# The end of the experts and the first tiles of dense attention rearranged, with result-row gathers that skip rows outside their class

## The reference, cut to what matters

```python
# first layer, feed-forward: 32 experts, 4 of them for each token, capacity 512
order = argsort(flat_ids); pos = arange(N) - starts[sorted_eid]
buf = zeros((E, C, 512)).at[sorted_eid, pos].set(x[tok], mode='drop')
g, u = split(einsum('ech,ehf->ecf', buf, w13))
eo = einsum('eci,eih->ech', silu(g) * u, w2)
routed = zeros_like(x).at[tok].add(eo[sorted_eid, pos] * flat_w[order][:, None])
shared = silu(x @ shared_gate_w) * (x @ shared_up_w) @ shared_down_w
x = x + routed + shared                     # beside the residual of its input norm
# second layer: q, k, v of 16 heads of 128, causal softmax, output projection
x = x + attention(layernorm(x), W_Q, W_K, W_V, W_O, b_Q, b_K, b_V, b_O)
```

## Time and profile before

| | us |
|---|---|
| Median of 3 runs | 3078.67 |
| Their range | 3078.39 to 3084.72 |
| The traced execution, its own time | 3087.53 |
| Its span, first to last instruction | 3086.1 |
| Mean granted TensorE clock | 0.967 |
| PE busy, share of the span | 94% |

### The profile page before, as it was taken

One profiled execution on the slowest core, in us unless ns is written; L12 is line 12 of the kernel. 1 busy time (PEld: TensorE's weight loads), 2 busy tenths in 40 slices (PEclk: granted clock), 3 DMA queues, 4 the chain that ended last, 5 costly groups with the idle time before them and its releaser, 6 DMA issues.

```text
span 3086.1 us, 46590 instructions
## 1 busy us (share of the span) xinstructions
PE 2887.0 (94%) x16712; PEld 1971.4 (64%) x16745; DVE 2055.0 (67%) x3792; ACT 1595.0 (52%) x2971; POOL 1138.1 (37%) x1152
## 2 busy tenths in 40 slices
PE   8899998899998889999996999999999999989998
PEld 3344443444443548888865888888888888856665
DVE  3554445699986877777776445656555566549998
ACT  2223222288887537777752444444456455437764
POOL 2343243334422033333345445454544444323310
PEclk9899999799999889999997999999999999989999
DMA  3000000000000238865673013222122234120000
GB/s 132 1 1 1 1 1 1 8 6 6 3 2 21 80 139 331 326 247 192 213 222 98 21 32 84 63 57 68 49 90 88 81 115 134 35 89 8 15 15 21
DMA packets 125913, 238.83 MB, mean 77 GB/s; under 512 B 14283, under 2 KB 73248, under 8 KB 119285
## 3 DMA queue, kind: packets, MB, share of 16 engines
q1 hardware_dynamic: 102020, 119.95, 12.1%
q0 software_dynamic: 22512, 113.80, 10.7%
q10 hardware_dynamic: 1152, 2.10, 0.2%
HBM read 223.99 MB, written 40.63 MB: 86 GB/s over the span
## 4 chain that ended last, share of the span: by engine, by line
PE 55%; DVE 13%; issue 7%; ACT 6%; POOL 3%; DMA 1%; SPq 0%; POOLq 0%; ACTq 0%; DVEq 0%; another core or an unknown queue 0%
PE ps L1651 9%; PE ps L1653 9%; PE ps L1652 9%; PE ps L901 3%; PE ps L890 3%; PE ps L2918 2%; DVE ps L2493 2%; PE ps L879 2%; PE ps L2928 2%; DVE b_mx L1023 1%; PE ps L2893 1%; ACT d_PTh L2355 1%; PE ps L1665 1%; ACT d_qk L2340 1%; DVE d_PTl L2507 1%
## 5 line engine op out<-in xcount | busy, mean ns | idle before, releaser
L2693 POOL TENSOR_SCALAR d_P<-d_P,d_rv 128x128 f32<-128x128 f32 (+3 forms) x256 | 289.8, 1144 | 553.2 <-DVE d_rv L2500 552.9
L1023 DVE TENSOR_REDUCE b_mx<-ps 128x1 f32<-128x512 f32 x512 | 320.8, 683 | 31.7 <-PE ps L879 28.1
L964 ACT ACTIVATE b_PT<-ps 128x512 f32<-128x512 f32 x512 | 277.6, 601 | 45.0 <-PE ps L890 43.5
L2348 ACT ACTIVATE d_P<-ps,d_nb 128x128 f32<-128x128 f32 (+3 forms) x256 | 135.2, 528 | 219.0 <-DVE d_nb L2493 217.7
L2507 DVE TENSOR_TENSOR d_PTl<-ps,d_PTh 128x384 fp32r<-128x384 f32 (+1 forms) x192 | 114.6, 597 | 157.4 <-ACT d_PTh L2355 157.4
L1651 PE MATMUL ps<-d_xh,d_wh 128*128 128x512 f32 x512 | 210.1, 410 | 1.5 <-DVE d_xl L2467 1.4
L1652 PE MATMUL ps<-d_xl,d_wh 128*128 128x512 f32 x512 | 204.1, 399 | 0.0
L1653 PE MATMUL ps<-d_xh,d_wl 128*128 128x512 f32 x512 | 203.9, 398 | 0.0
L879 PE MATMUL ps<-b_KT,b_Q 64*128 64x512 f32 x512 | 201.0, 475 | 2.1 <-DVE b_mx L1023 1.0
L890 PE MATMUL ps<-b_Q,b_KT 64*128 64x512 f32 x512 | 187.1, 452 | 0.5
L476 ACT ACTIVATE a_P<-ps 128x2048 f32<-128x2048 f32 (+1 forms) x48 | 76.4, 1592 | 210.0 <-PE ps L340 183.0
(11 more groups left out here) (485 smaller groups left out, 8456.3 us busy)
## 6 DMA issues: line engine op xcount, KB each, us to landing
eoscr<-x_eo SPq DMA_DIRECT2D x87, 256.0 KB, 4.3
d_w<-in_L_attn_W_Q SPq DMA_DIRECT2D x32, 256.0 KB, 3.9
d_w<-in_L_attn_W_K SPq DMA_DIRECT2D x32, 256.0 KB, 4.7
d_w<-in_L_attn_W_V SPq DMA_DIRECT2D x32, 256.0 KB, 5.4
d_wo<-in_L_attn_W_O SPq DMA_DIRECT2D x16, 512.0 KB, 4.7
d_cmb<-in_wgT SPq DMA_DIRECT2D x16, 512.0 KB, 5.0
d_cmb<-in_wuT SPq DMA_DIRECT2D x16, 512.0 KB, 4.7
d_cmb<-in_wdT SPq DMA_DIRECT2D x16, 512.0 KB, 4.2
```

What stands on the lines that cost most here:

```text
L964: e.activation(M.PT[:, half, v % 2, 2 * p + y, :], ps[:, O.bank(("ex", v, y)), :], ACT.Exp, scale=0.25).then_inc(S["b_ex"], 1)
L1023: e.tensor_reduce(M.mx[:, r % 2, q, h:h + 1], ps[:, O.SCORES[O.score(t, h) % 3], :], AX.X, ALU.max).then_inc(S["b_mx"], 1)
L2693: e.tensor_scalar(P, P, M.rv[:, y, q:q + 1], None, ALU.mult).then_inc(S["d_nm"], 1)
```

## The change

Index handling: `late_rows` adds 65536 to each index that is outside its class (`M.far`), and each of the 21 class gathers gets a bounds check, so that rows out of bounds are left out. As rows that are left out keep what the buffer holds, POOL sets the first early buffer to 0 at the start of the experts.

Order at the experts' end: on PE, the second half of `shared_up(1)` goes behind `down(94)`. On ACT, `split_dense(2)` and `shared(1)` come ahead of `leave(93)` and `leave(94)`. On DVE, `combine(0)` stays, `combine(1)` and `split_dense(0)` come ahead of `turn_act(94)`, and `shared(0)`, `combine(2)`, `split_dense(1)`, `split_dense(2)`, `shared(1)` follow.

Seam: POOL drains and counts itself as arrived before its three late gathers, and issues three of tile 3's four gathers behind them, also ahead of the wait for `G.go`, into another part of `DW.w`.

Dense stage: DVE adds tile 3's rows in one piece and takes its statistics ahead of `turn_x(2)`. POOL issues the fourth gather behind `rstd(0)` and spreads the gathers of tiles 4 and 5 between the `rstd`s. SP's next weights wait for `d_cb` 4, that is for tile 3 added.

```diff
-def stage_end(nc, G, S, last=False):
+def stage_end(nc, G, S, last=False, arrived=()):
     for e in (nc.tensor, nc.scalar, nc.vector, nc.gpsimd):
-        e.drain().then_inc(G.arrived, 1)
+        if e not in arrived:
+            e.drain().then_inc(G.arrived, 1)
...
+def own_rows_of(DW, k):
+    return DW.w[:, k, 2:4, :].rearrange("p k n -> p (k n)")
...                                        # expert_pe
-    def shared_up(f):
+    def shared_up(f, half):
...
-        if 0 <= j - (NTILE - 1) < 2:
-            shared_up(j - (NTILE - 1))
+        if j == NTILE - 1:
+            shared_up(0, 0)
+            shared_up(0, 1)
+        elif j >= NTILE:
+            shared_up(1, j - NTILE)
...                                        # expert_act
-    for j in range(NTILE + 3):
+    for j in range(NTILE + 1):
...
-        if 0 <= j - NTILE < 2:
-            shared(j - NTILE)
+        if j == NTILE:
+            shared(0)
...
+    split_dense(2)
+    shared(1)
+    leave(NTILE - 2)
+    leave(NTILE - 1)
...                                        # expert_dve, late_rows
+        e.tensor_scalar(M.far[:, 3, :, :], M.mk[:, 0, :, :], -FAR, FAR, ALU.mult, ALU.add)
...
+            t = dv.inc(e.tensor_reduce(M.far[:, 0, c, 0:LATE], M.mk[:, 1 + c, :, :], AX.X, ALU.add))
+        e.wait_ge(dv.sem, t)
+        t = dv.inc(e.tensor_scalar(M.far[:, 1, :, 0:LATE], M.far[:, 0, :, 0:LATE], -FAR, FAR, ALU.mult, ALU.add))
         e.wait_ge(dv.sem, t)
-        e.tensor_copy(G.GA[:, :, :], M.pr[:, 0, :, :])
-        e.tensor_copy(G.GL[:, :, :], M.sm[:, :, :]).then_inc(S["x_late"], 1)
+        e.tensor_tensor(G.GA[:, :, :], M.pr[:, 0, :, :], M.far[:, 3, :, :], ALU.add)
+        e.tensor_tensor(G.GL[:, :, :], M.sm[:, :, :], M.far[:, 1, :, 0:LATE], ALU.add).then_inc(S["x_late"], 1)
...                                        # expert_dve, order
-    for j in range(NTILE + 2):
+    for j in range(NTILE + 1):
...
+        if j == NTILE:
+            split_dense(0)
+            combine(1)
         if 0 <= j - 1 < NTILE:
             turn_act(j - 1)
-        if 94 <= j < 97:
-            combine(j - 94)
-        if j >= 95:
-            split_dense(j - 95)
-            shared(j - 95)
+        if j == NTILE - 1:
+            combine(0)
+    shared(0)
+    combine(2)
+    split_dense(1)
     split_dense(2)
+    shared(1)
...                                        # expert_pool; bounds_check also in early and last
     fetch(4)
+    e.memset(M.early[0], 0.0).then_inc(S["x_er0"], 1)
...
+    e.drain().then_inc(G.arrived, 1)
     for t in range(LATE):
         e.indirect_dma_start(out=late_rows_of(DW, t), out_offset=None, in_=eoscr,
-                             in_offset=bass.IndirectOffsetOnAxis(ap=G.GL[:, 2, t:t + 1], axis=0)).then_inc(G.late[t], 16)
+                             in_offset=bass.IndirectOffsetOnAxis(ap=G.GL[:, 2, t:t + 1], axis=0),
+                             bounds_check=128 * NTILE - 1, oob_is_err=False).then_inc(G.late[t], 16)
+    for k in range(3):
+        e.indirect_dma_start(out=own_rows_of(DW, k), out_offset=None, in_=eoscr,
+                             in_offset=bass.IndirectOffsetOnAxis(ap=G.GI[:, 3, k:k + 1], axis=0)).then_inc(G.own3, 16)
...                                        # dense_sp
-            e.wait_ge(S["d_cb"], 3)
+            e.wait_ge(S["d_cb"], 4)
...                                        # dense_dve
     norm(2)
-    combine(3, (0, 1))
+    combine(3)
+    stats(3)
     turn_x(2)
-    combine(3, (2, 3))
-    stats(3)
     project("v", 0)
...                                        # dense_pool
-    fetch(3, (0,))
     rstd(0)
-    fetch(3, (1, 2))
+    fetch(3, (3,))
     rstd(1)
-    fetch(3, (3,))
+    fetch(4, (0, 1))
     rstd(2)
-    fetch(4)
+    fetch(4, (2, 3))
+    fetch(5, (0, 1))
     rstd(3)
-    fetch(5)
+    fetch(5, (2, 3))
```

More of the change, by code:

```diff
@@ L1694, in turn_act @@
         i.then_inc(S["x_at"], 1)
-    def shared_up(f):
[L1697 to L1705, removed]
+    def shared_up(f, half):
+        if half == 0:
+            e.wait_ge(S["x_hT"], 32)
+            if f == 0:
+                e.wait_ge(S["x_XL"], NTILE)
+            else:
+                e.wait_ge(S["x_ag"], NTILE)
+        w, r = ((W.wg, 2 - 2 * f), (W.wu, 3 - 2 * f))[half]
+        for k in range(4):
+            t = e.matmul(ps[:, r, :], w[:, k, f * 128:f * 128 + 128], W.hT[k], start=k == 0, stop=k == 3)
+        t.then_inc(S["x_sgu"], 1)
     def shared_down(t_i):
@@ L1909, in early @@
     def early(t):
-        if t:
+        if t == 0:
+            e.wait_ge(S["x_er0"], 1)
+        else:
             e.wait_ge(S["x_wh"], 3 * (60 + t))
@@ L1914, in early @@
             e.indirect_dma_start(out=M.early[t][:, k, :], out_offset=None, in_=eoscr[0:128 * T_EARLY, :],
-                                 in_offset=bass.IndirectOffsetOnAxis(ap=G.GA[:, t, k:k + 1], axis=0)).then_inc(S[f"x_ga{t}"], 16)
+                                 in_offset=bass.IndirectOffsetOnAxis(ap=G.GA[:, t, k:k + 1], axis=0),
+                                 bounds_check=128 * T_EARLY - 1, oob_is_err=False).then_inc(S[f"x_ga{t}"], 16)
     def last(c, end):
@@ L1919, in last @@
             e.indirect_dma_start(out=M.last[3 * c + t], out_offset=None, in_=eoscr[0:128 * end, :],
-                                 in_offset=bass.IndirectOffsetOnAxis(ap=G.GL[:, c, t:t + 1], axis=0)).then_inc(S[f"x_gb{c}"], 16)
+                                 in_offset=bass.IndirectOffsetOnAxis(ap=G.GL[:, c, t:t + 1], axis=0),
+                                 bounds_check=128 * end - 1, oob_is_err=False).then_inc(S[f"x_gb{c}"], 16)
     fetch(4)
+    e.memset(M.early[0], 0.0).then_inc(S["x_er0"], 1)
     for j in range(NTILE):
@@ L2440, in combine @@
                 e.wait_ge(dv.sem, combine.last)
+            elif t == 3:
+                e.wait_ge(G.own3, 64)
             else:
@@ L2443, in combine @@
                 e.wait_ge(S[sem], n)
-            u = e.scalar_tensor_tensor(out=G.X[:, t, :], in0=dense_rows(M, t, k), scalar=G.Wt[:, t, k:k + 1], in1=G.X[:, t, :], op0=ALU.mult, op1=ALU.add)
+            src = own_rows_of(W, k) if t == 3 and k < 3 else dense_rows(M, t, k)
+            u = e.scalar_tensor_tensor(out=G.X[:, t, :], in0=src, scalar=G.Wt[:, t, k:k + 1], in1=G.X[:, t, :], op0=ALU.mult, op1=ALU.add)
             if k < 3:
@@ L2658, in fetch @@
         for k in rows:
+            landed = G.own3 if t == 3 else S[dense_landed(t)[0]]
             e.indirect_dma_start(out=dense_rows(M, t, k), out_offset=None, in_=eoscr,
-                                 in_offset=bass.IndirectOffsetOnAxis(ap=G.GI[:, t, k:k + 1], axis=0)).then_inc(S[dense_landed(t)[0]], 16)
+                                 in_offset=bass.IndirectOffsetOnAxis(ap=G.GI[:, t, k:k + 1], axis=0)).then_inc(landed, 16)
     def rstd(t):
@@ L3224, in build @@
         G.late = [nc.alloc_semaphore(name=f"late{t}") for t in range(LATE)]
+        G.own3 = nc.alloc_semaphore(name="own3")
         G.ps = root.enter_context(nc.psum_tensor("ps", [128, 8, 512], F32))
@@ L3267, in build @@
             expert_pool(nc.gpsimd, SM, a, M, W, DW, G, hscr, eoscr)
-        stage_end(nc, G, SM)
+        stage_end(nc, G, SM, arrived=(nc.gpsimd,))
         with later as ctx:
```

3 lines of the change are left out of this document (2 added, 1 removed).

## The result

The kernel after the change takes 3077.93 us (median of 20 executions, 3072.10 to 3083.94). The kernel before, run beside it 20 times, takes 3084.40 (3078.39 to 3094.44). The ratio is 0.998 with a 95% interval of 0.9972 to 0.9987: the interval lies clear of 1, so the kernel after is faster, by 6.5 us by the medians. Forecast were a gain of 7.7 and a time of 3071.0, within 3067.5 to 3077.0. The gain came 1.2 short of it by the medians, and the time lies 0.9 above the range.

A forecast was written before the change was run, and what follows sets the result against it. The bound was PE's idle gap between experts and dense attention, made by POOL's late barrier arrival and the dense stage's start. Gains of 5.1 before the value projection and 2.6 before the query projection, 7.7, gave 3071.0 us, range 3067.5 to 3077.0.

The forecast's parts named there:

- The bound: TensorE is 94% busy; time can be won only at the seam between experts and dense attention.
- Tile 94 earlier: Experts' end: half of shared_up(1) behind down(94) brings down(94) and its store 3.43 earlier; combine(1) ends at 1601.5.
- POOL's drain: Experts' end: 6.0 counted from the last gather's end, so the drain ends at 1615.4, between 1611.8 and 1617.2.
- the norms: Dense stage: norms on DVE might hold up POOL's gathers or roots, giving back 1.8 at most; left out of the sum.
- Six gathers, then the root: Behind POOL's drain: six gathers take 7.6, POOL is free at 1623.0, then the root; 5.1 gained before the value projection.
- POOL holds the seam again: Rival at the seam: longer drain or gathers of 1.6 each; gain 3 to 6.1, time 3072.6 to 3075.7; chance 0.22.
- Tile 3: Dense stage: adding tile 3 ahead of turn_x(2) takes 2.6 out of the chain to norm(3), before the query projection.
- Fewer rows: Bounds-checked gathers: moving fewer rows can only help the landing; no gain on the path was counted.
- The clock: Rival at the query projection: shorter gap keeps the upper clock, 2.3 more; gain 10, time 3068.7; chance 0.08.
- the forecast is 3078.67 - 7.7: Whole kernel: the gain of 7.7 taken from the median of the runs, 3078.67, gives 3071.0.

The follow-up runs named there:

- order only: The kernel before with only the new order of PE, ACT and DVE at the experts' end; 3078.64 against 3080.75 us, ratio 0.9991.
- arrival only: The kernel before with only POOL's drain moved ahead of its three late gathers; 3080.35 against 3080.75 us, ratio 0.9997.
- bounds only: The kernel before with only the bounds checks, new index handling and memset, in the old orders; 3082.11 against 3084.29 us, ratio 0.9992.
- dense only: The kernel before with tile 3 combined in one piece ahead of turn_x(2) and SP's next weights behind it; 3078.99 against 3080.98 us, ratio 0.9993.
- loads later: The changed kernel with SP's loads of dense biases and first output weights moved to the dense stage's start; 3071.77 us against 3080.98 before, ratio 0.9972.
- the changed kernel again: The changed kernel without any edit, timed again beside the kernel before; 3075.54 against 3080.75 us, ratio 0.9983.
- no bounds: The changed kernel without bounds checks, shifted indices and memset, so every gather moves all rows; 3080.66 us against 3080.98 before, ratio 0.9997.

## Why the prediction was right and where it was wrong

**The bound.** Right. All of the change's gain is in the one gap that was named: dense 6.3 shorter, seam 5.87, and the part after the query projection the same to 0.4.

**Tile 94 earlier.** Right. ACT's store is 3.2 earlier against PE's last product (-3.46, before -0.26). combine(1) waits for nothing: it starts at 1595.93 and ends at 1599.04, 1601.6 on the old scale, where 1601.5 was forecast, and down(94) starts at 1602.49. combine(2), now behind turn_act(94), waits 2.33 for its rows (1602.30 above), which delays nothing of PE.

**POOL's drain.** Its end was forecast at 1615.4 and is 1617.2 on the old scale, the far end of the range given. The step that failed is "I take 6.0 from the last gather's end". That the distance reads 5.9 in the kernel after is luck: over the nine traces with this drain it is 5.1 to 10.6. What the drain goes by is its own start or the last transfer of POOL's queue (last section). In the kernel after, that transfer is at +2.8 and the drain ends 3.1 behind it. In the second trace of this kernel the last gather ends 0.2 earlier, and the drain still at +5.9. I had also let only the store come forward with tile 94. SP's loads wait for the same tile and came forward with it, by 3.2 to 3.3, into the transfers of the class gathers; moving these loads away brings the drain's end 1.9 forward.

I also left the 18 class gathers where they were. In the changed kernel the last of them ends at +0.0 in place of -1.85, and at -0.2 in its second trace. All 18 take 25.9 and 26.2 in place of 24.6. The checks are not the cause: they add 0.05 each, and the kernel with the checks alone has 19.5 of busy time in them as before. It is the new order. The rows above show it: beside the split of the dense weights (1605.33, two SBUF operands) a gather takes 1.62, beside combine(2) (1602.30) 1.11 and 1.27, the others among them 1.00. In all twelve traces from 1560 to 1640, the 82 gathers of result rows with no DVE work beside them take 0.94 to 1.00, and the 11 beside this split alone 1.61 to 1.62. More of DVE's work of this kind now lies beside the gathers: the 18 are busy for 19.3 to 19.7 in all in the four traces with the old order, with and without checks, and for 19.9 to 21.3 in the eight with the new one, the lowest of them order only. The Trainium skill states this in "SBUF — State Buffer", section "Who interferes with whom": a DVE instruction with two inputs in SBUF contends with a GpSimd instruction that reads SBUF. The trace agrees with it. The prediction cited the other half of that section, on the norms: none of the three gathers that ran beside a norm in the kernel after was held up (0.99 to 1.01; 1626.38, 0.99, beside the norm at 1626.23), and no root ran beside one.

**Restart.** Not priced: 0.8 from the drain's end to the first gather. With the gathers' 1.84 and 0.08 less drain, POOL's late gathers start at 1618.0 on the old scale, 2.6 behind the forecast.

**Six gathers, then the root.** Right: 7.4 for 7.6, and the root comes the moment POOL is free, at 1625.4 (1623.0 forecast). From there the chain runs as worked out, and V is at 1631.9 in place of 1629.6. So the gain ahead of it is 2.7, not 5.1, and the gap on PE is 8.41, not 5, and the query projection starts 24.2 behind the last product's end, where 20 to 24 were named. This is the rival "POOL holds the seam again": its price was put at a gain of 3 to 6.1, and the seam's is 5.87. Of its two conditions the first, "The drain takes its 6.0 from its own start or more", came true: POOL gets to its drain at +0.0, 1611.2 on the old scale, and the drain ends 5.9 later. The second did not (no gather of the six over 1.00).

**Tile 3.** Right in mechanism, undersized: 3.1, not 2.6. Before, the first half of combine(3) waited 3.11 for its rows, until 1638.28, beside the loads of the next weights (DMA share 1.11 in 1636 to 1640). I had counted the chain from turn_x(2) on alone.

**Fewer rows.** "Fewer rows to move can only help the landing, of which nothing on the path is made here": the direction was right, the second half of the sentence wrong. Late rows land in 2.6 in place of 4.3. Above all the drain waits for what POOL has queued. Without the checks the gain is 2.3 in place of 5.9.

**The parts, alone and together.** Alone they are worth 2.15 (arrival), 1.98 (order), 2.23 (bounds) and 3.38 (dense), 9.7 together; the whole change gives 5.87. Of the difference of 3.9, 3.0 is the clock that rose in the value projection of the first three and not in the kernel after. The other 0.9 is overlap of the parts.

**The clock.** The rival did not happen. The clock is 0.50 in the first 4 us of the query projection after the change too, and its matmuls are the same 0.43 apart. The clock did move the seam elsewhere, within the value projection, by 1.0 in three of the experiments.

**The time.** The gain was 1.2 to 1.8 too high, and by itself that would have stayed within the range. The step that put the time outside it is "the forecast is 3078.67 - 7.7": the level came from three executions. Twenty give 3084.40 for the same kernel. The three are the first of these twenty. Beside the experiments, on three chips, its median was 3080.75 to 3084.29. From the level of 3084.40 the forecast's gain gives 3076.7, and the time measured is 1.2 away. The traced execution, at 3087.53, had said as much; I put its 8.9 down to "a difference of whole executions" and did not ask which of the two was the rare one. The range allowed for the gain's error only, which was 1.8 by the seam, and not for that of the level, which was 5.7.

## What to carry to other kernels

A drain on the engine that issues gathers was here also a wait for their transfers: before moving one, look at what is still under way on that queue, who else is using the DMA engines then, and count the restart. Where an order is changed on one engine, price again the instructions of its neighbours that run beside it, since a DVE instruction with two SBUF operands drew out POOL's gathers here (1.00 to 1.62). Ask too which transfers wait for the thing that is made earlier, and come earlier with it. And if the change is worth 0.2%, take the level from more than three executions, and judge each part by the seam in a trace, with the clock's share taken off.

## What the runs showed of the hardware

At the experts' end, POOL's drain has two floors, and the later of them decides in eight of the nine traces with such a drain, to 0.1. It ends no sooner than 5.1 after POOL gets to it (loads later 5.1 behind the last gather; with nothing queued, arrival only 5.1), and 3.0 to 3.1 behind the last movement on POOL's own queue. The ninth, bounds only, ends 5.4 after POOL gets to it and 4.4 behind that movement, 0.3 above both. In the kernel after, that movement and then the quiet look like this in windows of 1 us; the drain ends at 1614.66:

```profile
1610.00:1611.00 1.00, 1.00 (x4) 0.42 (x3) 0.57 (x1) 0.00 (x0) 0.00 (x0) 1.00 0.88 324
1611.00:1612.00 1.00, 1.00 (x4) 0.52 (x3) 0.00 (x0) 0.00 (x0) 0.00 (x0) 1.00 0.16 54
1612.00:1613.00 1.00, 1.00 (x3) 0.39 (x3) 0.90 (x2) 0.00 (x0) 0.00 (x0) 1.00 0.00 0
```

In 1611 to 1612, POOL's queue moves packets until 1611.5. The same distance is 3.1 in the kernel before and in the changed kernel again, and 3.0 to 3.1 in dense only, order only and no bounds, while the distance to the last gather's end goes from 5.9 to 10.6 among these. That the drain is held by the transfers is shown by taking the rows away (10.6 to 5.9) and by taking SP's loads out of their way (1.9 earlier). What the drain does in its 5.1 is not known, and it does not take them everywhere: at the routing's end POOL's drain ends 0.6 behind its tensor work and 2.2 behind the last movement on its queue. So these floors are a reading of this one place.

Leaving rows out makes a gather no cheaper for POOL (1.00 against 0.95), but its landing falls from 4.3 to 2.6. Over all traces the late gathers land in 3.7 to 6.7 without the checks and in 2.5 to 2.7 with them.

Left open: why the clock rises within the value projection in three of the experiments and not in the others.
